# Graph network with three attention layers: one 28-word accumulator row per head, heads turned by VectorE's transposition, and unread matmuls ahead of the products

## The reference, cut to what matters

```python
N_NODES, DIM, HEADS, LAYERS = 6250, 96, 4, 3
def _gat_layer(x, src, dst, W, a_src, a_dst, b):
    h = (x @ W).reshape(N, H, C)                      # H = 4 heads, C = 24
    alpha_s = jnp.einsum('nhc,hc->nh', h, a_src)
    alpha_d = jnp.einsum('nhc,hc->nh', h, a_dst)
    e = jax.nn.leaky_relu(alpha_s[src] + alpha_d[dst], 0.2)
    m = jax.ops.segment_max(e, dst, num_segments=N)
    ex = jnp.exp(e - m[dst])
    den = jax.ops.segment_sum(ex, dst, num_segments=N)
    alpha = ex / (den[dst] + 1e-16)
    out = jax.ops.segment_sum(h[src] * alpha[:, :, None], dst, num_segments=N)
    return out.reshape(N, H * C) + b
x = _layernorm(x + L0(x, edges, edge_attr))           # edge network and a segment sum
y = x
for l in range(3):
    y = relu(_gat_layer(y, src, dst, W[l], att_src[l], att_dst[l], bias[l]))
x = _layernorm(x + y)
```

## Time and profile before

| | us |
|---|---|
| median of three runs | 8601.86 |
| the profiled execution | 8603.82 |
| its span, first to last instruction | 8601.9 |
| mean granted clock of TensorE, share of 2.4 GHz | 0.629 |

### The profile page before, as it was taken

How to read it: one execution, slowest core, us unless ns; L and a number is a source line. 1 busy time by engine, 2 the same in 40 slices (tenths; PEclk the granted TensorE clock), 3 DMA queues, 4 the chain that set the end, 5 groups by cost and what they waited for, 6 DMA issues and landing times. The chain is left out here.

```text
span 8601.9 us, 131191 instructions
## 1 busy us (share of the span) xinstructions
PE 5700.5 (66%) x27740; PEld 5045.6 (59%) x27740; DVE 4467.6 (52%) x11640; ACT 3999.8 (46%) x8993; POOL 6236.4 (72%) x6545
## 2 busy tenths in 40 slices
PE   6999997777566666666656666666665666666663
PEld 2488886666555555555545555555554555555553
DVE  8977765555544444444444444444454444444446
ACT  5755554444344444444434444444443444444443
POOL 3677777777577777777667777777757777777775
PEclk7555555555566666666666666666666666666666
DMA  5222222222122222222222222222222222222221
GB/s 161 65 49 49 49 48 46 47 46 46 36 42 42 42 42 42 42 42 42 37 44 42 42 42 42 42 42 42 42 38 42 42 42 42 42 42 42 42 42 32
DMA packets 290250, 394.16 MB, mean 46 GB/s; under 512 B 176392, under 2 KB 183960, under 8 KB 287984
## 3 DMA queue, kind: packets, MB, share of 16 engines
q0 software_dynamic: 206976, 330.75, 20.1%
q1 hardware_dynamic: 61176, 46.25, 2.2%
q10 hardware_dynamic: 22024, 16.47, 0.8%
HBM read 367.38 MB, written 25.63 MB: 46 GB/s over the span
## 5 line engine op out<-in xcount | busy, mean ns | idle before, releaser
L637 POOL DMA_INDIRECT store<-table_a,idx x4851 | 4615.1, 951 | 1556.5 <-issue 1463.3
L1286 PE MATMUL ps<-store,work 128*128 x9744 | 1769.7, 352 | 945.1 <-ACT work L1218 942.5
L1286 PEld LDWEIGHTS ps<-store,work 128*128 128x128 f32 x9744 | 1646.2, 262 | 1132.3 <-issue 1128.1
L1269 PE MATMUL ps<-ident,work 128*128 128x128 f32 x4872 | 1148.9, 409 | 1371.7 <-ACT work L1225 1371.1
L779 POOL DMA_INDIRECT store<-table_m,idx x1617 | 1532.8, 948 | 615.1 <-issue 478.8
L1225 ACT ACTIVATE work<-work,small 128x896 f32<-128x896 f32 x696 | 725.1, 1042 | 2415.4 <-DVE store L1143 2379.3
L1269 PEld LDWEIGHTS ps<-ident,work 128*128 128x128 f32 x4872 | 920.4, 215 | 1453.8 <-issue 1359.3
L1151 DVE CUSTOM_DVE_ANT_0 work<-work,ps 128x896 f32<-128x896 f32 x696 | 756.6, 1087 | 1231.3 <-issue 937.8
L1162 DVE SCALAR_TENSOR_TENSOR work<-dstf,store,select 128x224 f32 x696 | 314.0, 451 | 1891.4 <-SPq L600 1887.5
L1277 PE MATMUL ps<-ident,work 128*128 128x128 f32 x4872 | 1090.3, 395 | 111.8 <-DVE work L1172 111.8
L1277 PEld LDWEIGHTS ps<-ident,work 128*128 128x128 f32 x4872 | 980.6, 217 | 115.4 <-DVE work L1172 115.4
(11 more groups left out here) (251 smaller groups left out, 5029.8 us busy)
## 6 DMA issues: line engine op xcount, KB each, us to landing
store<-table_a,idx POOLq DMA_INDIRECT x4851
store<-table_m,idx POOLq DMA_INDIRECT x1617, 2.5
work<-edge_parts ACTq DMA_DIRECT2D x232, 45.5 KB
edge_parts<-store SPq DMA_DIRECT2D x6, 1617.0 KB, 11.5
work<-edge_parts SPq DMA_DIRECT2D x50, 192.0 KB
table_a<-work SPq DMA_DIRECT2D x12, 606.0 KB, 6.3
work<-table_b ACTq DMA_DIRECT2D x232, 12.0 KB
idx<-in_src_dram SPq DMA_DIRECT2D x116, 28.0 KB, 1.8
```

What stands on the lines that cost most here:

```text
L637: pool.indirect_dma_start(rows[:, k % RING, j, 0:width], None, table, bass.IndirectOffsetOnAxis(ap=idx[:, k // CHUNK, at:at + 1], axis=0)) ...
L1269: last = pe.transpose(ps[:, 4 + j // 4, (j % 4) * P:(j % 4 + 1) * P], prob[:, par, j, :], ident[:])
L1286: last = pe.matmul(ps[:, 6 + par, 0:D + 1], probT[:, par, j, :], rows_of(at("slot", 3))[:, j, 0:D + 1], start=(j == 0), stop=(j == TPG - 1))
```

## The change

A source row now holds, for each head, 24 channels and a one (`CW` = 25 words), then four logits: 104 words instead of 101; products are 108 columns wide instead of 105. An accumulator row is 28 words instead of 100. `parts` copies only the own head's 25 words, with one instruction for each head and window. The folding is gone: `normalise` multiplies the accumulators by the reciprocal divisors into `heads` (32 words per window) with all 128 partitions, and a VectorE transposition in 32 x 32 blocks writes them to `XH`, where partition 32h+c is channel c of head h. ReLU and bias run in place on `XH`, and the products take all 128 partitions against weights padded to the same layout, loaded in the setup block. TensorE issues 20 bf16 matmuls at the head of each middle block, into bank 7, that nothing reads. The first index chunks of a pass are loaded in the block before it. The first table block halves the sum between VectorE and ScalarE, clears fewer words and lets ScalarE copy every second product. The final block transposes `XH` back with TensorE, and VectorE adds the residual; GpSimd does nothing there.

```diff
-TW = D + 1 + H
+CW = C + 1
+DX = H * CW
+TW = DX + H
-ROW_A = D + 4
+ROW_A = C + 4
...
+        def first_indices(sp, of):
+            for b in range(2):
+                sp.dma_start(idx[:, b, :], src[:, b * IW:(b + 1) * IW]).then_inc(of[f"idx{b}"], 16)
+        def keep_clock(pe, n, bank_):
+            weights, moving = ident[:].bitcast(BF16)[:, 0:P], ident[:].bitcast(BF16).unsqueeze(1).broadcast_to([P, 2, 2 * P])
+            for _ in range(n):
+                pe.matmul(ps[:, bank_, :].rearrange("p (b n) -> p b n", b=2), weights, moving, start=True, stop=True)
...
-                    for c in range(2):
-                        load_indices(c, c)
...
                     for v in range(2):
-                        a = big[:, bass.ds(at("row", 4) + v * ROW_A, D + 1)]
+                        a = big[:, bass.ds(at("row", 4) + v * ROW_A, CW)]
                         last = dve.scalar_tensor_tensor(a, a, keep[:, par, v:v + 1], part_sums[:, par, v, :], ALU.mult, ALU.add)
...
                     for v in range(2):
-                        last = nc.scalar.activation(part_sums[:, par, v, :], ps[:, 6 + par, 0:D + 1], ACT.Copy,
-                                                    scale=selects[:, bass.ds(at("table", 3) + WA + v, 1)])
+                        for h in range(H):
+                            of_head = slice(h * WA, (h + 1) * WA)
+                            last = nc.scalar.activation(part_sums[of_head, par, v, :], ps[of_head, 6 + par, h * CW:(h + 1) * CW], ACT.Copy,
+                                                        scale=selects[of_head, bass.ds(at("table", 3) + WA + v, 1)])
...
+        def normalise(dve, link, b0, b1):
+            w0, w1 = QUARTERS * tiles[b0][0], QUARTERS * (tiles[b1 - 1][-1] + 1)
+            r = rden[:, w0:w1]
+            link(dve.tensor_scalar(r, acc[:, w0:w1, C], 1e-16, None, ALU.add))
+            link(dve.reciprocal(r, r))
+            link(dve.scalar_tensor_tensor(r, acc[:, w0:w1, NEGMAX], FLOOR, r, ALU.is_lt, ALU.mult))
+            link(dve.tensor_tensor(heads[:, w0:w1, 0:C], acc[:, w0:w1, 0:C], r.unsqueeze(2).broadcast_to([P, w1 - w0, C]), ALU.mult))
+            return dve.transpose(XH[:, w0 * WA:w1 * WA], heads[:, w0:w1, :].rearrange("p w c -> p (w c)"))
+        PIECES = [(0, 1), (1, 4), (4, 7), (7, 10), (10, NB)]
+        WRITES = [(b, min(b + 2, NB - 1)) for b in range(0, NB - 5, 2)] + [(b, b + 1) for b in range(NB - 5, NB)]
...
             def _(act):
+                nc.scalar.activation(other_half, acc_m[0:D, HALF:N], ACT.Copy, accum_out=small[0:D, 41:42]).then_inc(s_half, 1)
...
-                link(dve.tensor_reduce(total, acc_m[0:D, 0:N], AX.X, ALU.add))
+                link(dve.tensor_reduce(total, acc_m[0:D, 0:HALF], AX.X, ALU.add))
+                dve.wait_ge(s_half, 1)
+                link(dve.tensor_tensor(total, total, small[0:D, 41:42], ALU.add))
...
-                pool.memset(big, 0.0).then_inc(s_zero, 1)
+                pool.memset(acc[:, :, C:], 0.0).then_inc(s_zero, 1)
+                pool.memset(heads[:, :, C:], 0.0)
...
                     def relu(b):
-                        act.wait_ge(b_sems["s_turn"], b + 1)
...
+                        act.wait_ge(b_sems["s_fold"], piece_of[b] + 1)
+                        v = XH[:, tiles[b][0] * P:(tiles[b][-1] + 1) * P]
+                        nc.scalar.activation(v, v, ACT.Relu, bias=bias_l[:, 0:1]).then_inc(b_sems["s_x"], 1)
...
-                    divisors(dve, b_sems["s_rden"])
-                    for c in range(NCH):
-                        fold(dve, c, range(QUARTERS - 1)).then_inc(b_sems["s_fold"], 1)
+                    for b0, b1 in PIECES:
+                        normalise(dve, link, b0, b1).then_inc(b_sems["s_fold"], 1)
...
+                    keep_clock(pe, 20, 7)
                     pe.wait_ge(b_sems["s_weights"], 1)
+                    for b in range(NB):
+                        pe.wait_ge(b_sems["s_x"], b + 1)
+                        if b >= 8:
+                            pe.wait_ge(b_sems["s_stage"], b - 7)
+                        product(pe, b, 0, 8, XH, w_l[:], b_sems["s_product"])
...
+        ENDS = [(0, 1), (1, 4), (4, 7), (7, 10), (10, 12), (12, NB)]
...
+                for b in range(NB):
+                    pe.wait_ge(s_relu, b + 1)
...
+                    for t in ts:
+                        last = pe.transpose(ps[:, b % 8, (t - ts[0]) * P:(t - ts[0] + 1) * P], XH[:, t * P:(t + 1) * P], ident[:])
...
+                    for b in range(*ENDS[p]):
+                        dve.wait_ge(s_back, b + 1)
+                        a = xn[:, ts[0]:ts[-1] + 1, :].rearrange("p t (h c) -> p (t h) c", c=C)
+                        dve.tensor_tensor(a, a, ps[:, b % 8, 0:len(ts) * P].rearrange("p (k c) -> p k c", c=WA)[:, :, 0:C], ALU.add).then_inc(s_res, 1)
```

## The result

Both kernels ran on the same chip: 8602.99 us before and 8709.21 after (medians of four runs each), a ratio of 1.0125, 95% interval 1.0107 to 1.0142. The change makes the kernel slower by 106 us, against a forecast of 83 us faster. The profiled execution of the changed kernel has a span of 8716.1 us, 114.2 more than before.

A forecast was written before the change was run, and what follows sets the result against it. GpSimd's gathers were taken to bound the kernel, untouched by the change; only time between passes could move. 12.9 + 43.7 + 29.7 - 3.6 = 82.7 us off 8603.8 gave 8521.1, forecast as 8520, range 8502 to 8560.

The forecast's parts named there:

- First table block, 13 less: First table block: halved node sum, smaller clearing that ends L1449's stall, and index load off the path save 12.9 us.
- Middle blocks, 22 less each: Two middle blocks: normalise and transposition replace folding, indices load earlier; 22.9 and 20.8 us less, 43.7 together.
- rival (a): Middle blocks: TensorE stays at half clock during the products; 10 us each, 8540 us in all; chance 0.22.
- Final block, 30 less: Final block: folds and waits beside GpSimd go, normalise and 13 additions come; 29.7 us less.
- rival (b): VectorE transpositions are dear: 19 us per extra ns an element, 8540 at twice the price; chance 0.08 mild, 0.02 beyond 5.4 ns.
- The passes, 4 more: Passes: eight `parts` copies add 1.15 us, within 2.07 us of slack; only drains lengthen, 1.2 us a pass, 3.6 together.
- rival (c): Passes: eight copies use up the slack; beyond 2.07 us added, each us costs 348; slower than before; chance 0.07.

The follow-up runs named there:

- the kernel of the 1.47 us copies: Changed kernel with its eight scaled copies over all 128 partitions each, only head 0's place read (own-head selection left out): 8548.7 us, 0.9932 of before.
- the four unscaled copies: Changed kernel with four unscaled copies for eight; VectorE multiplies both rows by the decay between landing and mask addition: 8622.9 us, 1.0041 of before.
- that of the two: Changed kernel with two copies of 25 words over all 128 partitions for the eight, heads' selection left out: 8474.4 us, 0.9864 of before.
- lead 3: Changed kernel in which GpSimd may start group g once the mask of step g-4 is turned (lead 3 for 1): 8504.3 us, 0.9899 of before.

## Why the prediction was wrong

**First table block, 13 less.** Right. The halved sum takes 3.90 us (3.8 forecast), the stall of 8.89 is gone, and the first gather is 12.0 earlier though the message pass ended 0.75 later in this execution.

**Middle blocks, 22 less each.** Right in sum: 21.7 and 22.2 (22.9 and 20.8 forecast). The 20 matmuls took 6.22 us (8 forecast) and the clock was 1.00 from then on, so rival (a) did not come. But their cover was not needed: without them, in the one execution that there is, one block was 1.2 us longer and the other the same, where I had put 10. One cost was missed inside: the logits, 6.17 us, came to end last, where I had them done before the write.

**Final block, 30 less.** 32.1. The transposition's price, 1.06 ns an element and some 0.15, kills rival (b).

**The passes, 4 more: the step that failed.** They cost 202. As the prediction put it, "1.15 fits, so nothing is lost per step". Three faults lie in it:

- The size. Eight copies take 2.27 us, 1.71 more, at a pitch of 0.285 and not 0.2. I took the overlap from two copies on the same 128 partitions. The doubt stood in rival (c).
- The slack. I took 2.07 us from the mask's turning to the gather's start. But a gather that waits starts 0.80 after that turning, as the row at 5473.49 shows. Over all groups of the second pass before, the time from turning to the start of the next group but one has a median of 1.88 us; less 0.79 (its floor in the changed kernel, where GpSimd waits) 1.1 are free. Even with the right size, 1.71 against 2.07, I would have said that nothing is lost. And in every tenth group the same wait leaves only 0.2 us, since the second gather there needs 2.99 from the turning: with nearly my own size the kernel of the 1.47 us copies loses 20 us a pass, nearly all of it there. By rival (c)'s rule with the 1.1, and 0.15 back from the shorter accumulation, (1.71 - 0.15 - 1.1) x 348 = 160 us, against 178 measured; that this is near is partly luck, since the rule counts only waits at groups' starts, and these make 97.
- The place of VectorE. That its instructions for the mask lie within some 0.3 us of a gather's start, and that a gather which starts while one of them runs is held up, stood in no term. It gave 30 us where the accumulation got shorter; it took 137 in the three passes where an instruction was added (gathering of the four unscaled copies against that of the two). Of the changed kernel's 178 us, 97 are late starts of groups, 36 the late second gathers of the tenth groups, and 45 longer gathers; these last are set off by the waits, since lead 3 took them away too.

The other 24 us of the 202 lie in the drains, and the copies make these too: six more in the kernel before lengthen its drains by 20 us. I had put 3.6 there. The range was too narrow for (c): its price is steep past the bound, 348 us for each us, and the bound was the least certain number in the working.

## What to carry to other kernels

The slack of a wait ends not where the waiting instruction starts but a signal's time before it; take that time (0.8 us here) from a row in which the engine really waits, and look at the tightest group, not the usual one (every tenth had 0.2 us free where the others had 1.1). Where a bounding engine runs on a fixed beat, look at what the engine beside it does at each beat's start (VectorE's instructions for the mask here): an edit that made these 0.2 us earlier or 1.0 later, inside the slack of every wait, cost 3 and 7% here. And before a costly stage is made cheaper, ask whether the bounding engine may run a group or two further ahead: a lead of 3 for 1 took the ratio from 1.0125 to 0.9899 in one line.

## What the runs showed of the hardware

Scaled copies of 25 words on ScalarE follow one another in 0.17 us when they use the same 128 partitions and in 0.285 when each uses another 32; unscaled ones on 32 partitions take 0.18 each. A gather that starts while a VectorE addition of two SBUF operands runs ends 0.82 us after it, if it starts 0.05 us or more behind the addition's start (so does one that starts during the 0.27 us multiplication L1169, with one SBUF tensor). If it starts 0.04 behind or less, it keeps its 0.94 and the addition is up to 0.08 longer. An addition that starts 0.08 us behind the gather's start delays neither. A gather that waits for TensorE's last transposition starts 0.80 us after its end. In the groups 16, 26 and so on the second gather starts 2.98 after it at the earliest (49 of the 66 such groups of the changed kernel, 35.9 us late in all); with lead 3 that is hidden, and what sets the period of ten stays open.
